# Attention's end merged with the node tables, one more gathered tile, and a window loop without the parity step, in a two-layer graph network

## The reference, cut to what matters

```python
h = x @ kernel                                            # layer 1
scores = leaky_relu(concat(h[src], h[dst]) @ attention)   # slope 0.2
e = exp(clip(scores, -2, 2))
out = segment_sum(h[dst] * (e / (segment_sum(e, src)[src] + 1e-7)), src)
x = layernorm(x + out)
m = relu(concat(x[src], x[dst]) @ Wm1 + bm1)              # layer 2, per edge
m = relu(m @ Wm2 + bm2) @ Wm3 + bm3
agg = segment_sum(m, dst) / max(count, 1)
x = layernorm(x + x + relu(concat(x, agg) @ Wn1 + bn1) @ Wn2 + bn2)
```

## Time and profile before

| | us |
|---|---|
| median of 3 runs | 2087.48 |
| lowest, highest | 2086.47, 2088.56 |
| profiled execution | 2091.26 |
| its span, first to last instruction | 2089.4 |

### The profile page before, as it was taken

The page is one execution under the profiler, slowest core; times in us unless marked ns, Lnnn a source line. Parts: engine busy times, 40 slices in busy tenths (PEclk is TensorE's granted clock), DMA queues, the critical chain, the costliest instruction groups (busy, mean ns, idle before and its releaser), DMA issues.

```text
span 2089.4 us, 54564 instructions
## 1 busy us (share of the span) xinstructions
PE 1704.9 (82%) x15385; PEld 1471.7 (70%) x15386; DVE 1578.3 (76%) x3406; ACT 1246.3 (60%) x2301; POOL 1157.0 (55%) x1189
## 2 busy tenths in 40 slices
PE   4467777766666667562899999999999999999986
PEld 3345666655555555520799999999999999999974
DVE  4578878766555566742788888888888888888886
ACT  3014566667777777233566766666666666666651
POOL 3212355445555545110777777777777777777730
PEclk9799998888887888766899999999999999999999
DMA  2112333433344444113544445444444444455421
GB/s 73 30 37 70 93 104 109 114 109 114 111 120 121 124 117 122 40 63 108 158 138 139 138 137 138 139 137 138 140 139 138 138 139 138 138 138 139 137 60 31
DMA packets 138294, 235.98 MB, mean 113 GB/s; under 512 B 24569, under 2 KB 89165, under 8 KB 138230
## 3 DMA queue, kind: packets, MB, share of 16 engines
q0 software_dynamic: 49632, 142.89, 24.2%
q1 hardware_dynamic: 88598, 92.44, 15.1%
HBM read 185.52 MB, written 10.66 MB: 94 GB/s over the span
## 4 chain that ended last, share of the span: by engine, by line
PE 51%; DVE 1%; ACT 0%; issue 0%; DMA 0%; DVEq 0%; SPq 0%
PE ps L1207 9%; PE ps L1206 9%; PE ps L1212 9%; PE ps L1190 8%; PE psA L1224 6%; PE ps L1185 4%; PE ps L1198 4%; PE ps L946 1%; PE ps L957 0%; PE ps L954 0%; PE psA L965 0%; DVE x L1018 0%; ACT u L979 0%; DMA bias<-in_L_gnn_bm 0%; DVE stats L1029 0%
## 5 line engine op out<-in xcount | busy, mean ns | idle before, releaser
L1161 POOL DMA_INDIRECT ga<-table_a,idx x784 | 778.6, 993 | 240.3 <-issue 181.0
L1206 PE MATMUL ps<-wm_hi,h_hi 128*128 128x256 f32 x1568 | 422.4, 303 | 0.2 <-ACT h_hi L1257 0.2
L1261 ACT ACTIVATE h<-ps 128x512 bf16<-128x512 f32 x392 | 234.1, 597 | 285.6 <-PE ps L1212 285.6
L1207 PE MATMUL ps<-wm_lo,h_hi 128*128 128x256 f32 x1568 | 386.2, 280 | 0.0
L514 POOL DMA_INDIRECT head_n<-scr_eye,row_at x250 | 290.4, 1162 | 140.8 <-POOL row_at L510 99.1
L1347 DVE SCALAR_TENSOR_TENSOR rest<-ps,h 128x512 f32<-128x512 f32 x392 | 269.6, 688 | 123.6 <-ACT h L1261 120.9
L1206 PEld LDWEIGHTS ps<-wm_hi,h_hi 128*128 128x128 f32 x1568 | 294.5, 188 | 23.6 <-ACT h_hi L1257 1.2
L1207 PEld LDWEIGHTS ps<-wm_lo,h_hi 128*128 128x128 f32 x1568 | 295.4, 188 | 1.5
L557 PE MATMUL psC<-ring_n,ring_m 128*126 x1180 | 242.6, 339 | 53.8 <-DVE ring_n L680 29.6
L611 ACT ACTIVATE stage<-psC 126x626 f32<-126x626 f32 x125 | 86.2, 689 | 303.5 <-PE psC L566 301.1
L1341 DVE SCALAR_TENSOR_TENSOR h_lo<-ps,h_hi 128x512 fp32r<-128x512 f32 x392 | 264.5, 692 | 2.3 <-ACT h_hi L1257 2.3
(11 more groups left out here) (188 smaller groups left out, 2749.2 us busy)
## 6 DMA issues: line engine op xcount, KB each, us to landing
cnt<-stage SPq DMA_DIRECT2D x125, 305.2 KB
dstb<-scr_dst SPq DMA_DIRECT2D x196, 126.0 KB
ga<-table_a,idx POOLq DMA_INDIRECT x784, 2.9
bw<-table_b SPq DMA_DIRECT2D x196, 63.0 KB
table_b<-b_st SPq DMA_DIRECT2D x12, 375.0 KB
head_n<-scr_eye,row_at POOLq DMA_INDIRECT x250, 4.1
table_a<-a_st SPq DMA_DIRECT2D x12, 250.0 KB
x<-in_x SPq DMA_DIRECT2D x1, 1562.5 KB
```

The lines of the kernel that those rows point to most:

```text
L1161: pool.indirect_dma_start(ga[:, u, k, :], None, table_a, bass.IndirectOffsetOnAxis(ap=idx[:, u, k:k + 1], axis=0)).then_inc(gathered[u][k] ...
L1206: pe.matmul(ps2[q][:, t % 2, :], hi, w_hi[:, k, :], start=False, stop=True, skip_group_check=True)
L1207: pe.matmul(ps2[q][:, t % 2, :], hi, w_lo[:, k, :], start=False, stop=True, skip_group_check=True)
```

## The change

The functions `attention` and `node_tables` become one block, with `layernorm` done by chunk, so that the tables of the first chunks are made while later ones are summed. Its staging slots (`NB = 3`), `spread`, and the weights lie over tiles that are free by then. The last subtraction for table b and `spread` move to POOL, the zero rows to `index_tables`, the clearing of `T.agg` to ACT at the start of `messages`. In the window loop three tiles are gathered (`GATHERED = 3`), the head is four tiles, `weigh` and the second part of `leaky` stand one window later, and the loop's bounds themselves point into the shifted copy of the keys, for which `T.edge_keys` gets a shifted copy too.

```diff
-GATHERED = 2
+GATHERED = 3
 HEAD = GATHERED + 1
-BANKS_AT = (0, 0, 0, 1, 1, 1, 1, 1, 2, 2)
+BANKS_AT = (0, 0, 0, 0, 1, 1, 1, 2, 2, 2)
-WEIGH_AT = (1, 3)
-LEAKY_AT = (1, 2)
+WEIGH_AT = (2, 4)
+LEAKY_AT = (1, 3)
@@ index_tables
+            pool.memset(zpad[:, :], 0.0).then_inc(zpad_ready, 1)
...
             sp.dma_start(scr_eye.rearrange("(k p) n -> p k n", p=BLK), eye[:, :, :]).then_inc(eye_out, 16)
+            sp.wait_ge(zpad_ready, 1)
+            sp.dma_start(table_b[N:NPAD, :], zpad[:, :]).then_inc(zpad_out, 16)
             sp.wait_ge(eye_out, 16)
             sp.wait_ge(dst16_out, 16)
+            sp.wait_ge(zpad_out, 16)
...
+            step(dve.tensor_copy(T.edge_keys[:, 2, 0:KEYS - 1], T.edge_keys[:, 1, 1:KEYS]))
@@ attention, windows
-                    with eng.Fori(first + HEAD, end, TPT) as n:
+                    low, high = first + HEAD, end
+                    if shifted:
+                        odd = eng.snap((low & 1) * (KEYS - 1), min_val=0, max_val=KEYS - 1)
+                        low, high = low + odd, high + odd
+                    with eng.Fori(low, high, TPT) as n:
@@ attention, hot_rows
-                keys = block_keys[:, (v + 1) % 2, bass.ds(n + (n & 1) * (KEYS - 1), tiles)].rearrange("p (o s) -> p o s", o=1)
-                iota = T.iota_m if tiles == TPT else T.iota_h
-                return dve.tensor_tensor(at, iota[:, u, :, :], keys.broadcast_to([P, WME, tiles]), ALU.is_equal)
+                keys = block_keys[:, (v + 1) % 2, bass.ds(n, tiles)].rearrange("p (o s) -> p o s", o=1)
+                iota = T.iota_m[:, u, :].rearrange("p (m o) -> p m o", o=1)
+                return dve.tensor_tensor(at, iota.broadcast_to([P, WME, tiles]), keys.broadcast_to([P, WME, tiles]), ALU.is_equal)
@@ attention, after the window loop: tensor
+            for c in range(2):
+                sum_chunk(TURNS_A, 0, c)
+            pe.wait_ge(loaded, 32)
             for c in range(CH):
-                sum_chunk(TURNS_A, 0, c)
+                if c + 2 < CH:
+                    sum_chunk(TURNS_A, 0, c + 2)
+                pe.wait_ge(rows_ready, c + 1)
...                                       # transposes of the chunk, wait for their copy
+                for g in pairs_of(c):
+                    if g >= 2:
+                        pe.wait_ge(rest_ready[0], g - 1)
...                                       # two products per block with Wm1, then a part of spread
@@ attention, after the window loop: scalar
+            for c in range(CH + 3):
+                for g in pairs_of(c - 3):
+                    s, i = g % NB, len(pair(g))
+                    act.wait_ge(rest_ready[1], g + 1)
+                    act.activation(b_st[:, s, 0:i, 2, :], rest[:, s, 0:i, :], ACT.Copy).then_inc(part_ready[2], 1)
...                                       # sqrt of c, copies of c - 1, part 1 of pairs_of(c - 2)
+                for g in pairs_of(c - 1):
+                    s, i = g % NB, len(pair(g))
+                    act.wait_ge(ab_done, g + 1)
+                    if g >= NB:
+                        act.wait_ge(b_out[s], 16 * (g // NB))
+                    act.activation(b_st[:, s, 0:i, 0, :], psC[g % 2][0:BLK, 1, 0:i * H].rearrange("p (b h) -> p b h", h=H), ACT.Copy).then_inc(part_ready[0], 1)
@@ attention, after the window loop: vector
+            for c in range(CH + 2):
+                if c < CH:
+                    sums(c)
+                if 1 <= c <= CH:
+                    normalise(c - 1)
+                for g in pairs_of(c - 2):
+                    tables(g)
@@ messages, scalar, ahead of the sweeps
+            agg_flat = T.agg[:, :, :].rearrange("p k n -> p (k n)")
+            act.activation(agg_flat, T.ident[:, 0:1].broadcast_to([P, 2 * NPAD]), ACT.Copy, scale=0.0).then_inc(agg_cleared, 1)
```

362 lines of the change are left out of this document (163 added, 199 removed).

## The result

The changed kernel takes 2155.99 us (median of 4 runs, 2148.57 to 2160.72) where the kernel before, in the same comparison, takes 2088.02. The ratio is 1.0322, with a 95% interval of 1.0291 to 1.0352: slower by 3.2%, and outside the range of 2020 to 2094. The profiled execution has a span of 2157.8 us against 2089.4, 68.4 more.

A forecast was written before the change was run, and what follows sets the result against it. VectorE was taken to bound the first five spans, no engine the other 20, and stores the tables. Terms -27 + 0 - 6 + 3.3 + 2.6 = -27 took 2087.5 to 2060.5 us, range 2020 to 2094.

The forecast's parts named there:

- First five spans, -27: Counting loop, first five spans: fewer passes and less parity arithmetic, against longer heads, give -27 us (-10 to -36).
- 17.2 for the parity arithmetic: First five spans: 143 remaining passes each lose 0.12 us of VectorE address arithmetic, 17.2 us gained.
- rival C: First five spans: the 0.35 us gap is PE's, so 17 is not won; 2077.5 us, chance 0.10.
- 16.0 less 6: First five spans: 13 passes of 1.23 us go, 16.0 gained; 25 longer head tables cost 6.
- Other twenty spans, 0: Counting loop, last 20 spans: POOL's third gather fills its idle time, so no change, 0 us (-26 to +49).
- Rival E: Late spans: POOL's chain decides, third gather issued 1.5 us later with two buffers; +49, 2109.5 us, chance 0.13.
- Rival D: Late spans: more port locks stall POOL, 1.01 us per window now, a quarter more is 25; 2085.5 us, chance 0.12.
- The later `weigh` holds up nobody: Late spans: moving `weigh` a window later delays nothing, since its PE reader moves too and SyncE waits later.
- Attention's end and tables, -6: End of attention and node tables: merged stage starts stores 27 us earlier, mostly handed back to the store ring; -6 us.
- VectorE's first add stays: Start of the merged tail: VectorE's first add stays at 862.5 us, as the waits ahead of it are older.
- Setup, +3.3: Setup: one more VectorE copy (0.65 us) and the zero pad's store (some 2.6) add 3.3 us (0.6 to 4).
- message start, +2.6: Start of messages: ACT's 5.9 us clearing of `agg` delays the gathers, in part covered; +2.6 us (0 to 5.9).

The follow-up runs named there:

- e5: Kernel before with one row of `iota_m` per window spread over the tiles by a zero step; 1.002 of the kernel before, late spans 546.2 us against 545.5.
- e6: Kernel before with loop bounds carrying the shift into the second key table, dense tables kept; 1.0027 of the kernel before, late spans 552.8 us against 545.5.
- e3: Kernel before with three gathered tiles (`GATHERED = 3`) alone; 2114.24 us, 1.0113 of the kernel before.
- e8: Changed kernel with four buffers instead of two for gathered rows and their row numbers; 1.0017 of the kernel before, late spans 559.6 us against 616.7.
- e9: Changed kernel with `weigh` and `leaky` in the loop reading their second operand from PSUM, result not the kernel's; late spans 593.8 us against 616.7.
- e7: Kernel before with only the new places of `weigh`, `leaky` and the chunk sums; 1.0043 of the kernel before, late spans 546.7 us against 545.5.
- e13: Kernel before with the new places and the shifted keys, dense tables, two gathered tiles; 1.0155 of the kernel before, late spans 579.4 us.
- e1: Changed kernel with two gathered tiles instead of three; 2117.1 us, 1.0141 of the kernel before.
- e2: Changed kernel with the old places of `weigh`, `leaky` and the chunk sums; 2130.55 us, 1.0219 of the kernel before.
- e4: Kernel before with only the merged end of attention, zero pad stored in the setup and `agg` cleared by ScalarE; 2087.06 us, 0.9987 of the kernel before.
- e11: Kernel before with merged tail, four buffers, three gathered tiles and the zero pad stored early in the setup; 2078.26 us, 0.9962 of the kernel before.
- e16: Kernel before with merged tail, early pad store, four buffers, three gathered tiles and `low` behind window 0's stage copy; 2054.55 us, 0.9842 of the kernel before.

## Why the prediction was wrong

**What bounds the kernel.** Right for the late spans in that no engine was full and the counts were waited for. Wrong for the first five, where "bound by VectorE" failed: the earlier trace rows shows a pause put down to issue, and I took it for VectorE's own arithmetic. e5 and e6 show that TensorE's pass sets the 1.23 in the long windows.

**First five spans, -27.** Measured -4.2. The step that failed is the 17.2 for the parity arithmetic: it won 2.0 (e6), as in rival C. The 13 passes won 10.6 (e3), and that agrees with 16.0 less 6 by luck: in e3 the longer heads cost nothing, for with the dense tables 504 elements take 0.415 us as 378 do (0.418). So the passes won two thirds of the 16.0. Only with the zero step is a head longer, 0.68 for its 504 elements, 0.26 more than before; "no faster mode to lose" read the rate off 252 and 378 elements alone. Passes and arithmetic together would be 12.6. With four buffers the changed kernel has 236.2 there, which is -10.6; with two it has 242.6. So the two-deep ring took 6.4 of the gain in these spans, though only beside the other edits: e3 has two buffers and 236.2.

**Other twenty spans, 0.** Measured +71 to +72. This is the step that made the prediction wrong, and it has three failures. (1) GpSimd's idle sum of 149.4 was read as time to give. I set a sum of busy time against a sum of idle time, but idle time of an engine in a two-deep ring is latency, not room: the window's chain of gathers and landing grew, and TensorE waited for its end. e3 gives +38.6 for this alone, and e8 shows that depth mends it. Rival E had the mechanism ("the third is issued 1.5 later, and the buffers are two") and 49 as its price; I gave it 0.13 because of the idle sum. (2) Rival D, more locks, counted GpSimd's stalls: 1.01 per window, and a quarter more for 25 us. With the means of the changed kernel they are 0.22 for the copy and 3 x 0.32 for the gathers, 1.18, so two thirds of that quarter came. The 22.9 of e9 are all that `weigh` and `leaky` cost by locks, the old ones too; how much of them is new no run shows. D and E were priced as alternatives, and they are no alternatives: both occurred. (3) "The later `weigh` holds up nobody" is true alone (e7, +1.2), and false beside the shifted keys (e13, +33.9 instead of 8.5). I costed each edit on the kernel before, one at a time, and a loop whose waits keep its engines in step doesn't add up that way. From what single edits showed, the sum would be 38.6 + 7.3 + 1.2 + 0.7 = 47.8; the kernel lost 71.2. Taken out of the changed kernel one at a time, the third gather gives back 47.5 (e1) and the new places 22.3 (e2).

A fourth failure didn't move the forecast, which took no gain here, but weakened its arguments: 23 passes went and not 48, so VectorE had 28 us less to do (23 x 1.23) and not 59. "Excluded for the passes, which follow from the edge list" was the wrong thing to be sure of.

The forecast that `leaky` would wait for `low` came true (VectorE waits for it in 15 of the late spans, 55.5 us in all). That the spans would be steadier was wrong: 36.0 and 29.1 stand where 28.7 and 26.8 stood.

**Attention's end and tables, -6.** Measured -3.4 by stretch. The rounds came as forecast. The issues of table b on the DMA queue, pairs 3 to 6, and a part 0 that waits for such a store:

```profile
984.78 0.27 SPq L541 DMA_DIRECT2D table_b<-cnt  x1
...
994.50 0.27 SPq L541 DMA_DIRECT2D table_b<-cnt  x1
...
995.63 0.45 SPq L541 DMA_DIRECT2D table_b<-cnt  x1
...
1008.82 0.27 SPq L541 DMA_DIRECT2D table_b<-cnt  x1
...
ACT cnt L749 <- DMA table_b<-cnt: 27.8, 6, 6.2
```

(The sum behind the -6 has a slip, 889 + 80.2 is 969.2 and not 968.4.) A round of one pair takes 9.7 (9.1 forecast), a round of two 14.3 (14.6), and part 0 waits for `table_b`, 27.8 us in six rounds. What failed is "VectorE's first add stays": it stands 6.3 behind the start of `weigh` (935.35 - 929.00), where it stood 5.2 behind it (862.5 - 857.3). The two parts of `weigh` take 4.69 instead of 3.48, since GpSimd's `spread` lies across them:

```profile
924.92 5.43 POOL L581 TENSOR_TENSOR pr<-node_inv,ident 25x3125 f32<-25x3125 f32 x1 [9.20 <-DVE node_inv L829]
...
929.00 4.69 DVE L784 TENSOR_TENSOR pr<-pr,cnt 125x1875 f32<-125x1875 f32 x2 [4.23 <-DMA cnt<-stage]
```

`spread` ends at 930.35, 1.35 after `weigh` began, which is about the 1.21 lost. I had looked at the port only as VectorE keeping GpSimd out; here it seems to have gone the other way, by this one place and no run of its own.

**Setup, +3.3, and message start, +2.6.** The setup came out at 3.6. The copy put the store of the eye 0.67 later (49.77 against 49.10), as forecast. For the pad e4 shows 2.4, near the 2.6, and e11 shows that the store costs about as much at the other place on SyncE's queue. The messages started their products 11.5 after the block began, before 11.9 after: gathers start 4.6 later (1063.58 - 1057.1 = 6.5 against 1.9), but TensorE's first product waits in both kernels for VectorE's `hot_e`, which ends 11.8 behind the block's start before and 11.5 after. Behind it TensorE still waits 1.06 for gathered rows (at 1070.74), and from the block's start to the end the two kernels differ by 0.1. So the cover that I called partial was all but complete.

**The rivals and what would show it.** Of "spans of 27, 29 would be E" the changed kernel has 29.1 and 36.0. "Part 0 waiting for `table_b`" and "9 and 15 us" held. "Passes of 1.11 (1.23: C)" gave 1.17 in the changed kernel. For these 0.06 less I have no account, since the pass in e5 and e6 is 1.22 to 1.25. The sign "POOL still waits over 50 us for PE in the late spans" came by a hair (52.6 in 309.1 to 929) and would have been no use: that wait fell from 143.5 while the spans grew, and what grew was TensorE's wait for gathered rows, 51.9 to 117.0, for which I had put no sign. The range missed because E was priced for three gathers only, without the locks on top and without the turns.

## What to carry to other kernels

Idle time of an engine that feeds a ring is no room for more work: compare the latency of one slot (issue, work and landing of all its parts) with the ring's depth times the period, and try a deeper ring before anything is put into it. A pause put down to issue on one engine belongs to the slower partner of the handshake as long as nothing excludes it; see whether the partner has a pause of the same period. Edits that cost 8.5 us by themselves may cost 34 together (e13) when one moves a pause and the other takes away the wait that had let a second engine through. Count a loop's passes in the trace: windows that needed none had one. And where an engine pauses once in each turn of a long loop, look whether the instruction queue moved a packet in the pause.

## What the runs showed of the hardware

- A compare of int16 tables on VectorE takes 0.291, 0.418 and 0.415 us for 128x252, 128x378 and 128x504 when both operands are dense in the last axis (two, three and four tiles; kernel before and e3). With one operand spread there by a zero step it takes 0.42, 0.55 and 0.68 (e5 and the changed kernel). So the zero step costs 0.13, 0.13 and 0.26: with it each element costs 1.0 ns, and without it only half of that where the last axis has two or four.
- `weigh` and `leaky` with two SBUF operands lengthen a gather's issue on GpSimd from 1.01 to 1.26 us on average and once to 4.03; with the second operand in PSUM the longest of 265 was 1.65. Where a GpSimd `tensor_tensor` lay across `weigh`, that took 4.69 instead of 3.48.
- At each turn of the hardware loop VectorE pauses twice with no wait shown: 6.38 and 3.82 us in the kernel before (at 536.11 and 541.51), 3.54 and 5.03 in the changed one, 4.31 and 4.89 in e13. A packet of 8192 bytes of the instruction queue starts 2.0 to 2.9 us before the end of such a pause.
- When e5 to e8 ran, the kernel before took 2461.68 us instead of 2088. Setup, attention and tables of e5 to e8 were as fast as elsewhere; the message loop alone was slower, at a granted clock of 0.94 (e5, 1000 to 2400 us) against 1.00. It isn't a fixed property of a chip: under the same chip number, when e13 to e16 ran, the kernel before took 2087.1. Why is open.
- The issue of one store on SyncE, `table_b<-zpad`, took 2.14 us behind the store of the eye (e4) and 20.26 right behind the loads of the setup (e11); what stands behind it on SyncE waits as long.
